# Attention with the softmax denominators' reciprocals spread by a DMA round trip through DRAM in place of matmuls, and the steps' places set anew

## The reference

```
kv = concat([context, latents], axis=1)            # 1857 rows
q, k = rms_norm(latents @ Wq), rms_norm(kv @ Wk);  v = kv @ Wv
scores = einsum('bhgqd,bhkd->bhgqk', qg, k) * scale
probs = softmax(scores, axis=-1)
out = einsum('bhgqk,bhkd->bhgqd', probs, v)
```

## Time and profile before

| | us |
|---|---|
| median of 3 runs (3215.82 to 3217.71) | 3216.54 |
| the profiled execution's own time | 3211.71 |
| its span in the trace | 3209.9 |
| PE busy in it | 3026.6 (94%) |
| DVE busy | 2455.7 (77%) |
| ACT busy | 2052.9 (64%) |
| POOL busy | 1317.7 (41%) |
| mean granted TensorE clock | 0.976 of full speed |

### The profile page before, as it was taken

The page is one execution under the profiler, slowest core; times in us unless marked ns, Lnnn a source line. Parts: engine busy times, 40 slices in busy tenths (PEclk is TensorE's granted clock), DMA queues, the critical chain, the costliest instruction groups (busy, mean ns, idle before and its releaser), DMA issues. The chain is left out here.

```text
span 3209.9 us, 52293 instructions
## 1 busy us (share of the span) xinstructions
PE 3026.6 (94%) x14906; PEld 2470.7 (77%) x14906; DVE 2455.7 (77%) x3316; ACT 2052.9 (64%) x2899; POOL 1317.7 (41%) x791
## 2 busy tenths in 40 slices
PE   6996999999899999998999999999999997697899
PEld 5884888888778888886788888778888885585577
DVE  6773888888958888887788888868888888423765
ACT  3443777777857777876787777767777786311211
POOL 1330455555525555555355555535555555000000
PEclk9998999999999999999999999999999998898899
DMA  6873110011211100012111010211011000734300
GB/s 227 274 234 117 33 40 33 33 41 41 75 35 33 47 33 33 33 37 85 34 33 42 33 39 33 73 47 35 33 37 45 33 26 11 218 100 132 96 30 20
DMA packets 183911, 210.92 MB, mean 66 GB/s; under 512 B 10965, under 2 KB 125653, under 8 KB 182761
## 3 DMA queue, kind: packets, MB, share of 16 engines
q1 hardware_dynamic: 179016, 196.27, 19.0%
q0 software_dynamic: 2176, 8.39, 0.8%
q10 hardware_dynamic: 2592, 4.72, 0.5%
HBM read 140.14 MB, written 69.21 MB: 65 GB/s over the span
## 5 line engine op out<-in xcount | busy, mean ns | idle before, releaser
L870 POOL TENSOR_TENSOR att_sm<-att_sm,att_sc 128x1024 f32<-128x1024 f32 (+1 forms) x384 | 852.6, 2220 | 697.0 <-DVE att_pr L821 696.5
L676 PE MATMUL att_ppv<-att_pr,att_V 128*128 128x512 f32 (+1 forms) x2880 | 848.8, 404 | 22.8 <-DVE att_pr L821 20.1
L656 PE MATMUL att_pqk<-att_q,att_kT 128*128 128x512 f32 (+1 forms) x2880 | 850.1, 404 | 6.6 <-issue 3.8
L748 ACT ACTIVATE att_sc<-att_pqk,att_rk 128x512 f32<-128x512 f32 (+1 forms) x960 | 661.8, 690 | 188.6 <-PE att_pqk L656 185.5
L617 PE MATMUL att_pkv<-att_ctxT,att_wkv 128*128 128x512 f32 (+1 forms) x3072 | 756.3, 376 | 1.1 <-DVE att_kT L837 0.5
L821 DVE TENSOR_TENSOR att_pr<-att_sc,att_pr 128x1024 fp32r<-128x1024 f32 (+1 forms) x512 | 631.7, 1234 | 37.8 <-ACT att_pr L759 37.8
L617 PEld LDWEIGHTS att_pkv<-att_ctxT,att_wkv 128*128 128x128 f32 x3072 | 559.5, 189 | 120.6 <-DVE att_kT L837 1.2
L676 PEld LDWEIGHTS att_ppv<-att_pr,att_V 128*128 128x128 f32 (+1 forms) x2880 | 532.6, 191 | 149.3 <-DVE att_pr L821 35.1
L815 DVE TENSOR_TENSOR att_sc<-att_sc,att_pmax 128x1024 f32<-128x1024 f32 (+1 forms) x512 | 585.2, 1143 | 42.7 <-PE att_pmax L625 42.7
L656 PEld LDWEIGHTS att_pqk<-att_q,att_kT 128*128 128x128 f32 (+1 forms) x2880 | 505.8, 185 | 122.5 <-ACT att_sc L748 14.1
L759 ACT CAST att_pr<-att_sc 128x1024 fp32r<-128x1024 f32 (+1 forms) x512 | 511.2, 998 | 137.3 <-PE att_ppv L676 135.8
(11 more groups left out here) (130 smaller groups left out, 2749.9 us busy)
## 6 DMA issues: line engine op xcount, KB each, us to landing
q_scr<-pre_qT SPq DMA_DIRECT2D x128, 256.0 KB, 3.5
att_wkv<-kv_scr SPq DMA_DIRECT2D x64, 512.0 KB, 4.0
att_q<-q_scr SPq DMA_DIRECT2D x64, 512.0 KB, 4.3
o_scr<-att_on SPq DMA_DIRECT2D x64, 256.0 KB, 2.0
out_oraw<-o_scr SPq DMA_DIRECT2D x64, 256.0 KB, 4.9
att_sc<-in_ctx SPq DMA_DIRECT2D x16, 768.0 KB, 4.7
pre_wq_raw<-in_L_xattn_Wq SPq DMA_DIRECT2D x8, 1024.0 KB, 6.8
kv_scr<-pre_kv SPq DMA_DIRECT2D x8, 1024.0 KB, 7.6
```

The source lines that it names most:

```text
L656: mm = pe.matmul(pqk[0:m, (h * NT + t) % 2], kT[:, kp, t * P:t * P + m], q[:, qp, h], start=(i == 0), stop=(i == 2))
L676: mm = pe.matmul(ppv[:], V[0:m, vp, t], pr[0:m, pp, (t // 2) % NP, t % 2], start=(t == 0 and i == 0), stop=(t == NT - 1 and i == 2))
L748: act.activation(sc[0:m, h, t], pqk[0:m, s % 2], ACT.Copy, scale=rk[0:m, t:t + 1]).then_inc(sc_ok, 1)
L870: pool.tensor_tensor(sm[0:m, 0:w], sm[0:m, 0:w], sc[0:m, h, i:i + w], ALU.add).then_inc(sum_ok, w)
```

## The change

`db` is no longer a step of TensorE. The reciprocals in `rden` (now one buffer for each half) are stored to a DRAM scratch `rd` of 512 floats for each half by a new SyncE step `ds`, element by element in transposed order, and read back to all 128 partitions of a new SBUF tile `rdb` by the step `db`, now SyncE's, once the store has landed. `on` multiplies with `rdb` in place of `pred`. `mt` and the last `dt` wait for `den_ok` (the reduction has read `pred`) in place of `on_ok`. All places are replaced by a new set.

```
+        rd=nc.dram_tensor("rd_scr", [2, G * S // 2], F32, kind="Internal").ap(),
...
-        rden = sb("rden", [P, 4])
+        rden = sb("rden", [P, NH, 4])
+        rdb = sb("rdb", [P, HALF])
...
-        TILE = dict(copy=0.39, pv=24.5, sub=19.4, exp=21.0, hi=21.7, lo=22.4, sum=23.0, max=0.98)
-        END = dict(mt=(2.79, 0.69),
-                   red=(1.4, 0.7),
-                   mb=(5.2, 5.2),
-                   oraw=(23.4, 23.1),
-                   fold=(24.8, 23.1),
-                   dt=(24.67, 24.47),
-                   dred=(28.43, 26.63),
-                   db=(31.76, 40.56),
-                   on=(30.61, 30.51),
-                   st=(28.31, 28.31),
+        TILE = dict(copy=0.79, pv=24.5, sub=19.6, exp=21.0, hi=21.8, lo=22.4, sum=23.6, max=0.98)
+        END = dict(mt=(1.89, 0.99),
+                   red=(1.0, 0.8),
+                   mb=(5.3, 5.3),
+                   oraw=(23.2, 22.9),
+                   fold=(25.1, 24.7),
+                   dt=(24.47, 26.07),
+                   dred=(28.33, 25.73),
+                   ds=(25.73, 27.73),
+                   db=(28.63, 30.03),
+                   on=(32.53, 30.43),
+                   st=(31.73, 34.23),
                    ldq=(-29.9, -29.9))
-        CHUNK = (dict(k=(-12.68, -11.4, -10.76), v=(-1.68, -0.8, -0.46), khi=-10.76, klo=-10.23, kn=-6.46, var=-7.66, pow=-0.06, vhi=-1.36, vt=14.9, vthi=15.16, vtlo=15.24),
-                 dict(k=(-5.98, -5.2, -5.19), v=(6.6, 7.74, 8.52), khi=-3.46, klo=-3.13, kn=-0.16, var=0.44, pow=1.23, vhi=13.14, vt=16.8, vthi=17.26, vtlo=17.44),
-                 dict(k=(-4.21, -3.06, -2.67), v=(8.8, 13.12, 14.74), khi=-1.77, klo=-1.14, kn=3.64, var=2.73, pow=4.24, vhi=15.54, vt=21.9, vthi=21.06, vtlo=22.34),
-                 dict(k=(0.2, 0.24, 0.32), v=(20.0, 21.62, 22.64), khi=0.54, klo=1.17, kn=4.13, var=5.84, pow=6.54, vhi=22.24, vt=23.7, vthi=24.36, vtlo=24.54))
-        LOADS = dict(ldwk=-26.5, ldwv=-11.4)
+        CHUNK = (dict(k=(-12.28, -11.86, -11.1), v=(-1.38, -0.8, -0.46), khi=-10.96, klo=-10.63, kn=-6.36, var=-7.66, pow=-0.56, vhi=-0.96, vt=15.2, vthi=15.66, vtlo=15.44),
+                 dict(k=(-5.7, -4.38, -3.76), v=(6.0, 7.84, 8.6), khi=-3.76, klo=-3.53, kn=0.04, var=0.14, pow=1.03, vhi=14.74, vt=17.4, vthi=18.56, vtlo=18.34),
+                 dict(k=(-3.01, -2.09, -1.87), v=(8.62, 12.42, 13.24), khi=-1.77, klo=-1.64, kn=1.14, var=2.93, pow=4.74, vhi=15.54, vt=21.9, vthi=21.46, vtlo=21.74),
+                 dict(k=(0.12, 0.2, 0.44), v=(20.0, 22.22, 22.54), khi=0.14, klo=1.67, kn=4.33, var=4.64, pow=6.34, vhi=22.44, vt=23.9, vthi=24.16, vtlo=25.14))
+        LOADS = dict(ldwk=-30.6, ldwv=-15.2)
...
+                    elif what == "ds":
+                        sp.wait_ge(rden_ok, AHEAD + u + 1)
+                        sp.dma_start(scr["rd"][h].rearrange("(c p) -> p c", p=P), rden[:, h], allow_slow_non_contiguous=True).then_inc(rd_out, 16)
+                    elif what == "db":
+                        sp.wait_ge(rd_out, AHEAD + 16 * (u + 1))
+                        sp.dma_start(rdb[:], scr["rd"][h].partition_broadcast(P)).then_inc(rdb_in, 16)
...
                     elif what == "mt":
                         pe.wait_ge(max_ok, AHEAD + maxima(u, NT - 1))
-                        pe.wait_ge(on_ok, AHEAD + u - 1)
+                        pe.wait_ge(den_ok, AHEAD + u - 1)
...
                         if last and h == 1:
-                            pe.wait_ge(on_ok, AHEAD + u)
+                            pe.wait_ge(den_ok, AHEAD + u)
...
-                    elif what == "db":
-                        pe.wait_ge(rden_ok, AHEAD + u + 1)
-                        spread(pred, rden).then_inc(db_ps, 1)
...
-                        dve.wait_ge(db_ps, AHEAD + u)
-                        dve.reciprocal(rden[:], den[:]).then_inc(rden_ok, 1)
+                        dve.wait_ge(rd_out, AHEAD + 16 * (u - 1))
+                        dve.reciprocal(rden[:, h], den[:]).then_inc(rden_ok, 1)
                     elif what == "on":
-                        dve.wait_ge(db_ps, AHEAD + u + 1)
+                        dve.wait_ge(rdb_in, AHEAD + 16 * (u + 1))
                         dve.wait_ge(oraw_ok, AHEAD + u + 1)
                         dve.wait_ge(o_out, AHEAD + 16 * u)
-                        dve.tensor_tensor(on[:], oraw[:], pred[:], ALU.mult).then_inc(on_ok, 1)
+                        dve.tensor_tensor(on[:], oraw[:], rdb[:], ALU.mult).then_inc(on_ok, 1)
```

More of the change, by code:

```diff
@@ L420, in attend @@
         lat_in, wk_in, wv_in, o_out = sem("lat_in"), sem("wk_in"), sem("wv_in"), sem("o_out")
+        rd_out, rdb_in = sem("rd_out"), sem("rdb_in")
         x_in = [sem(f"x_in{i}") for i in range(4)]
@@ L425, in attend @@
                  "qk_ps sc_ok max_ok mt_ps red_ok mb_ps sub_ok exp_ok phi_ok plo_ok sum_ok pv_ps oraw_ok "
-                 "dt_ps den_ok rden_ok db_ps on_ok fold_ok").split()
+                 "dt_ps den_ok rden_ok on_ok fold_ok").split()
         loop_sems = [sem(n) for n in names]
@@ L429, in attend @@
          qk_ps, sc_ok, max_ok, mt_ps, red_ok, mb_ps, sub_ok, exp_ok, phi_ok, plo_ok, sum_ok, pv_ps, oraw_ok,
-         dt_ps, den_ok, rden_ok, db_ps, on_ok, fold_ok) = loop_sems
+         dt_ps, den_ok, rden_ok, on_ok, fold_ok) = loop_sems
         LAG = 24
-        TILE = dict(copy=0.39, pv=24.5, sub=19.4, exp=21.0, hi=21.7, lo=22.4, sum=23.0, max=0.98)
-        END = dict(mt=(2.79, 0.69),
-                   red=(1.4, 0.7),
-                   mb=(5.2, 5.2),
-                   oraw=(23.4, 23.1),
-                   fold=(24.8, 23.1),
-                   dt=(24.67, 24.47),
-                   dred=(28.43, 26.63),
-                   db=(31.76, 40.56),
-                   on=(30.61, 30.51),
-                   st=(28.31, 28.31),
-                   ldq=(-29.9, -29.9))
@@ L555, in _ @@
             def _(pool):
-                start_ahead(pool, loop_sems + [lat_in, wk_in, wv_in, o_out] + x_in + q_in)
+                start_ahead(pool, loop_sems + [lat_in, wk_in, wv_in, o_out, rd_out, rdb_in] + x_in + q_in)
                 identity(pool, ident, id_ok)
@@ L573, in step @@
                 def step(n, what, h, t, before=None, dn=0, last=False, xb=None, head=0, fresh=False):
+                    u = NH * n + h
                     if what in ("ldwk", "ldwv"):
```

## The result

The changed kernel takes 3370.61 us (median of 4 runs, 3361.69 to 3376.27) against 3216.18 before (4 runs, 3212.68 to 3217.71): slower, ratio 1.048 with a 95% interval of 1.0455 to 1.0505. The profiled execution took 3365.44 us, its span 3363.6, 153.7 more than the 3209.9 of before.

What follows compares the result with a forecast made beforehand. TensorE was taken to bound the kernel inside a batch. Removed matmuls -56.1, `mt`'s waits -4, boundaries +6 and tail +3.8 sum to -50.3 us: 3216.5 becomes 3166.2 us, with 8 in 10 for 3150 to 3200.

Steps and rivals of the forecast that it cites:

- What bounds the kernel: Inside a batch TensorE sets the pace: a unit takes 72.4 us, PE busy in all of it, VectorE in 62.0.
- the price of what was removed: Spreading matmuls on TensorE: 0.89 us for each set of 8, 63 sets in its stream, 56.1 us off.
- rival (b): Eight spreading matmuls cost less than read, 0.72 us a set; 63 sets give 10.7 us less: 3177 us; chance 0.05.
- The price of the store: Store of 512 single floats to DRAM: taken at 2.75 us, upper end 6.8 us.
- (c): Round trip outgrows its cover: gain eaten from a trip of 15.4 us on, 3319 us at 17; chance 0.08.
- The cover: Other work hiding the trip before `on`: 9.8 us in the first half, 10.8 in the second, against 6.0 needed.
- What stands behind a late `on`: First half: `max`, `sub`, `lo` 5 us ahead of `pv`; second: `var`, about 3.6 us free. DMAs cost 0 in the stream.
- Boundaries: At the three batch boundaries `on` comes late and VectorE stands: 0 to 3 us each, 2 taken, +6 in all.
- SyncE's queue: `db` of the first half is ahead of `ldwv` and not held; loads behind are needed later: cost 0.
- The tail: Last half of the attention, where nothing hides the round trip: +3.8 us, ends +2.9 and +9.3.
- Moved places: Other new places keep each producer ahead of its consumer: cost 0, up to 1 us a unit in the range.
- The signs of being wrong: `ds` of 7 us or more, `on` waiting for DMA in every half, or units above 71.5 us with PE waiting.

Runs made afterwards that it cites:

- no trip: Changed kernel without the store and the read-back; `on` multiplies by a tile of ones, so the division is left out: 3161.99 us, ratio 0.9835.
- the short trip: Changed kernel with reciprocals stored as 128 pieces of 16 B in place of 512 of 4 B, columns divided by wrong denominators: 3199.02 us, ratio 0.9945.
- the quick store: Changed kernel, whole computation, storing 128 pieces of 16 B, with transposes taking every fourth column of the sums: 3202.74 us, ratio 0.9961.

## Why the prediction was wrong, step by step

**What bounds the kernel, and the price of what was removed: right.** TensorE was the pace inside a batch; with no trip the unit is 70.57 us, against 70.6 worked out. That this kernel's 3162 us lie near the forecast of 3166 proves less, and is in part luck: the forecast has the trip's +6 and +3.8 in it. Without them it would be 3156; the 4 us expected from `mt`'s waits are in no run by themselves. The 0.89 us a set, read from starts, held; the lower price of the rival (b) would have left a unit at 71.0 (two sets of 0.72 off 72.4).

**The price of the store: the first step that failed.** It was put at 2.75 us, with 6.8 as the upper end, "the slowest row"; it took 8.2, to the read-back's issue. Both bounds came from rows whose pieces don't share 64 B of a DRAM target: the query stores write 512 B pieces, the single floats of the norm weights are read. (The norm weights were not the only loads of single floats either: two gates' loads of 0.5 KB took 2.8 and 3.8 us.) The nearest rows in kind were not near in the property that mattered. The count of 512 pieces, for which the step looked at the query stores, is harmless. With a slow store bounded only by rows of other layouts, the range should have reached to the deciding point of (c), and the chance of 0.08 was too low. The whole trip was put at 6.0 us with an end of 11.4, and took 13.1. But this step alone doesn't make the loss. With 13.1 us in the prediction's own terms the stream still loses nothing (late by 3.3 and 2.3 us, with 5 and 3.6 free), the tail costs 10.9 in place of 3.8, and the forecast becomes 3173 us. The kernel took 3371. The read-back was put at 2.9 and took 4.7, with an upper end of 4.3: from lines written just before 4.7 (floats) or 4.1 (16 B pieces), from a scratch written once at the start 3.1 to 3.2.

**The cover: nearly right.** 9.8 us for the first half; measured 13.06 - 3.99 = 9.1. For the second half 10.8 were taken and 11.8 measured: its `on` is late by only 0.9 to 1.5 us in the stream.

**What stands behind a late `on`: the second step that failed.** The cost in the stream was put at 0. For the first half the text named `max`, `sub` and `lo`, and 5 us of freedom. It missed `vtlo` of chunk 1 at 18.34, for which `v` of chunk 3 at 20.0 waits: 1.66 places, and 4 us of lateness already cost TensorE 1.2 to 4.6. Against no trip the stream lost 68 us. The rival (c) had the sign and the kind of mechanism right, but it didn't foresee this either: it counted the stream alone, with the same freedom, and a trip of 13.1 us costs nothing by it, as its deciding point was 15.4. The kernel lost 154 us at 13.1.

**The clock: no term.** That TensorE's matmuls take longer where it has stood (a clock of 0.50 behind the 11.3 us) was priced at nothing; this is 60 of the 204.6 us between the changed kernel and the one without a trip.

**Boundaries: right in kind, wrong in size, and the largest error.** +6 us in all were taken, with 3 each as the end; the three stretches are +96.7 together against before, and +111 against the run without a trip. That fewer steps lie between `dred` and `on` was said, but they were not counted. The `on` of the last half has none and waits 12.7 us, and the half whose store stands behind a context load waits 9.6 to 10.0. Even the short trip leaves some 35 us at boundaries and tail.

**SyncE's queue: right for the order in a batch.** `db` was not held. That the 8 us of a landing would themselves hold the loads behind was priced at nothing; it is 27 to 29 us.

**The tail.** +3.8 us with an end of +9.3: 12.76 - 2.17 = +10.6 for the last `on`, by the prices of store and read-back. The whole last stretch is +23.1.

**Moved places.** Cost 0 in the stream: right.

**The signs of being wrong: well chosen.** Of the three that the prediction named, all came: a `ds` of 7 us or more, `on` waiting for DMA in every half, and units above 71.5 us.

## What to carry to other kernels

A wait that is put in place of work is priced by its own latency and by the whole list of steps behind it on its engine, boundaries included, and a latency that no row shows is bounded by rows of the same layout and direction or left open to the point where it decides. A small store that another DMA is to read should be laid out so that each partition writes neighbouring bytes of its own; here that was an index change in four transposes, and worth 168 us. Where a round trip stands in for matmuls, the boundaries have to be counted first: here the largest part of the loss was there, what remained with the quick store was nearly all there, and an earlier start of the second half's trip brought 18 us.

## What the runs showed of the hardware

All of this is from SyncE's queue. 2 KB of single floats stored to DRAM, neighbouring floats from different partitions, land the later the more densely they lie: from issue to the read-back's issue 1.9 us at one float in 64 B, 2.6 at four, 3.7 at eight, 8.2 at sixteen. The packets themselves are through 1.3 us after the issue in each of these four runs; in the trace of the changed kernel the DMA engines then stand all but idle. 128 packed floats take 7.6 us, 128 packed pieces of 16 B 1.4. The unit of memory in which this happens, and its cause, are not shown. A broadcast read of 2 KB to 128 partitions took 4.7 us right behind the store of packed floats into the same memory, 4.1 behind the store of 16 B pieces, and 3.1 to 3.2 from memory written once at the start. TensorE's transposes of the sums, reading them with a stride of four floats, take 0.39 us for a set of four in place of 0.36.
